# Three stages of a transformer-block kernel rewritten: the key lookup written out for all 32 batches with its head sums on TensorE, the gate sums of the recurrence on VectorE, and one power per group in the slot stage

## The reference, cut to what matters

```python
def step(h, x_t):
    score = jnp.einsum('bsh,bh->bs', enc_hiddens, h @ W)
    attn = jax.nn.softmax(score, axis=-1)
    context = jnp.einsum('bs,bsh->bh', attn, enc_hiddens)
    gx = jnp.concatenate([x_t, context], axis=-1) @ kernel + bias
    gh = h @ recurrent_kernel
    z = sigmoid(xz + hz); r = sigmoid(xr + hr)
    cand = jnp.tanh(xh + r * hh)
    h_new = z * h + (1.0 - z) * cand
```

## Time and profile before

| | |
|---|---|
| median of 3 runs | 8622.68 us |
| the profiled execution: its time / its span | 8619.14 / 8617.3 us |
| PE busy | 6440.8 us (75%) |
| DVE busy | 5008.3 us (58%) |
| ACT / POOL busy | 2976.5 us (35%) / 810.9 us (9%) |
| slot stage, four passes from 43.55 us | about 740 us |
| key-lookup passes, 817.60 to 1420.00 us | 602.4 us |
| recurrence with its block ahead, 3204 to 4586 us | about 1382 us |
| mean granted clock of TensorE (1.00 is 2.4 GHz) | 0.807 |

### The profile page before, as it was taken

How to read it: one execution, slowest core, us unless ns; L and a number is a source line. 1 busy time by engine, 2 the same in 40 slices (tenths; PEclk the granted TensorE clock), 3 DMA queues, 4 the chain that set the end, 5 groups by cost and what they waited for, 6 DMA issues and landing times. The chain is left out here.

```text
span 8617.3 us, 210690 instructions
## 1 busy us (share of the span) xinstructions
PE 6440.8 (75%) x89337; PEld 4834.8 (56%) x89337; DVE 5008.3 (58%) x17660; ACT 2976.5 (35%) x5373; POOL 810.9 (9%) x755
## 2 busy tenths in 40 slices
PE   3443223989987668998997886888888888888875
PEld 2332112767765338888886664555655556555553
DVE  4444666455455666665564336757667575775742
ACT  2222111333332222111111113545545455554541
POOL 0111222000000010000000001111011110111100
PEclk7666556999998875555557998999999999999986
DMA  1000000000000000000000000000000000000000
GB/s 29 0 0 2 0 0 25 1 1 1 1 1 4 0 3 3 4 4 4 4 4 21 0 0 17 2 9 3 2 10 2 10 2 7 5 2 10 2 4 10
DMA packets 61248, 45.12 MB, mean 5 GB/s; under 512 B 22521, under 2 KB 56125, under 8 KB 60227
## 3 DMA queue, kind: packets, MB, share of 16 engines
q1 hardware_dynamic: 60355, 32.26, 1.4%
HBM read 30.14 MB, written 2.10 MB: 4 GB/s over the span
## 5 line engine op out<-in xcount | busy, mean ns | idle before, releaser
L367 DVE TENSOR_REDUCE peak<-ps 128x8 f32<-128x1024 f32 (+1 forms) x832 | 816.9, 1024 | 270.7 <-PE ps L289 269.6
L409 ACT ACTIVATE e<-ps,H_lowT_c 77x1024 f32<-77x1024 f32 x384 | 406.0, 1106 | 253.7 <-PE ps L313 253.7
L409 ACT ACTIVATE e<-ps,H_lowT_s 128x1024 f32<-128x1024 f32 x384 | 407.3, 1112 | 248.2 <-PE ps L313 248.2
L327 PEld LDWEIGHTS ps<-e,H_vt 128*32 128x32 f32 (+1 forms) x12288 | 318.1, 111 | 254.8 <-ACT e L409 135.0
L327 PE MATMUL ps<-e,H_vt 128*32 128x128 f32 (+1 forms) x12288 | 430.3, 280 | 23.7 <-DVE xs L387 17.7
L313 PE MATMUL ps<-H_qr,H_km 32*128 32x128 f32 (+1 forms) x12288 | 420.3, 275 | 0.0
L313 PEld LDWEIGHTS ps<-H_qr,H_km 32*128 32x128 f32 (+1 forms) x12288 | 406.9, 169 | 14.8 <-issue 1.0
L1737 PE MATMUL ps<-F_hp,F_encW 128*128 128x1 bf16 (+2 forms) x12288 | 368.7, 166 | 54.2 <-issue 52.2
L1737 PEld LDWEIGHTS ps<-F_hp,F_encW 128*128 128x128 bf16 x12288 | 347.7, 104 | 55.7 <-issue 55.7
L1895 ACT ACTIVATE F_ex<-ps,F_nm 16x77 f32<-16x77 f32 x256 | 81.7, 319 | 860.6 <-DVE F_nm L1815 860.6
L1776 PE MATMUL ps<-F_eT,F_ctxp 77*128 77x1 f16 (+1 forms) x12288 | 375.6, 165 | 0.0
(11 more groups left out here) (595 smaller groups left out, 14976.6 us busy)
## 6 DMA issues: line engine op xcount, KB each, us to landing
G_w<-in_L_ffn_w SPq DMA_DIRECT2D x16, 256.0 KB
H_f<-in_L_xcond_f_w SPq DMA_DIRECT2D x12, 256.0 KB
H_nw<-in_L_xcond_n_w SPq DMA_DIRECT2D x21, 128.0 KB, 2.2
A_cond<-in_cond SPq DMA_DIRECT2D x1, 2048.0 KB
out_x<-x_all SPq DMA_DIRECT2D x1, 2048.0 KB, 8.7
ctx_rows<-in_ctx SPq DMA_DIRECT2D x1, 1232.0 KB
D_wq<-in_L_xcond_attn_wq SPq DMA_DIRECT2D x2, 512.0 KB
D_wk<-in_L_xcond_attn_wk SPq DMA_DIRECT2D x2, 512.0 KB
```

Of the source, the lines that this page charges most:

```text
L327: last = nc.tensor.matmul(ps[PAD_COLS * s:PAD_COLS * (s + 1), FLAT, r * S:(r + 1) * S], vt_of(u)[0:keys, QUAD * r + s, :], e[0:keys, half, ...
L367: last = nc.vector.tensor_reduce(peak[:, HL * half:HL * (half + 1)], view, AX.X, ALU.max, negate=True)
L409: nc.scalar.activation(e[0:keys, half, :], ps[0:keys, AGAIN[half]:AGAIN[half] + 2, :].rearrange("p b t -> p (b t)"), ACT.Exp, bias=low(u) ...
```

## The change

- Slot stage: one power of 4 columns for each group instead of one of 8 for both; VectorE normalises both groups in all norms, and ScalarE none; the softmax is subtract (VectorE, 77x512), one exponential per group (ScalarE), and sum, reciprocal, multiply, add (VectorE, each over the whole group).
- Key lookup: one Block with all 32 batches written out; `lengths(N + 1)` stands ahead of `choose(N)` on VectorE and `invert(N + 1)` ahead of `multiply(N)` on GpSimd; the sum over heads is eight accumulating identity matmuls and one for the tail (`sum_heads`); layer norm, expert activations and residual of a group are placed inside the batches of its neighbours (`nT`, `act_g` twice).
- Recurrence: RUN is 32 (four passes); `of_token` goes, VectorE adds the token's part to the gates (`gate_sums`), one tanh of 32 columns makes both gates, the bias is added once in the block ahead; three `of_state` matmuls move ahead of `turn_weights`; GpSimd copies all token inputs into place; in the block ahead the weights' parts are split early and GpSimd clears `encW` last.

```diff
-                                nc.vector.tensor_scalar(veps2[0:rows], mv2[0:rows, :, :, 1], LN_EPS, None, ALU.add).then_inc(sem["var_ready"], 1)
-                                dve.wait_ge(sem["rstd_ready"], r + 1)
-                                for j in range(1 if shared else 2):
+                                for j in range(2):
+                                    nc.vector.tensor_scalar(vepss[j][0:rows], mvs[j][0:rows, :, 1], LN_EPS, None, ALU.add).then_inc(sem["var_ready"], 1)
+                                for j in range(2):
+                                    dve.wait_ge(sem["rstd_ready"], at(r, j))
...
-                                    for u in range(U):
-                                        last = nc.scalar.activation(attns[j][:, u, :], per(bank(j, 2))[0:CL, u, :], ACT.Exp, bias=ams[j][:, u:u + 1],
-                                                                    scale=float(D) ** 0.5, accum_out=ars[j][:, u:u + 1])
+                                    nc.scalar.activation(attns[j][:], attns[j][:], ACT.Exp, scale=float(D) ** 0.5).then_inc(sem["exp_done"], 1)
...
+                        def sum_heads(N):
+                            b = N % 2
+                            pe.wait_ge(sem["outer_ready"], N + 1)
+                            pe.wait_ge(sem["tail_ready"], N + 1)
+                            if N:
+                                pe.wait_ge(sem["expert_ready"], N)
+                            for h in range(QH):
+                                nc.tensor.matmul(ps[:, 7, 0:E], ident[:], outer[:, b, h].rearrange("p i k -> p (i k)"),
+                                                 start=(h == 0), stop=False, skip_group_check=True)
+                            nc.tensor.matmul(ps[:, 7, E - 1:E], ident[:], tail[:, b:b + 1], start=False, stop=True,
+                                             skip_group_check=True).then_inc(sem["coef_done"], 1)
...
+                        for N in range(B):
+                            g, u, b = at(N)
+                            if u == 2 and g + 1 < NG:
+                                prepare(g + 1)
+                            if N + 2 < B:
+                                scores(N + 2)
+                            if u == 0 and g:
+                                mix(g - 1)
+                            sum_heads(N)
...
-            RUN = 16
+            RUN = 32
...
-                                of_token(k)
                                 of_state(k, PRODUCTS[0:3])
                                 turn_scores(k)
                                 if k > 0:
                                     late(k - 1)
+                                of_state(k, PRODUCTS[3:4])
                                 turn_weights(k)
-                                of_state(k, PRODUCTS[3:6])
+                                of_state(k, PRODUCTS[4:6])
                                 attend(k)
...
+                            def gate_sums(k):
+                                t, c = k // CH, k % CH
...
+                                dve.wait_ge(sem["gate_done"], k + 1)
+                                nc.vector.tensor_tensor(gsum[:, c], ps[:, 4 * c + 3, 0:3 * CB].rearrange("p (i b) -> p i b", i=3),
+                                                        xloc[t // PART][:, t % PART, :, mine(c)], ALU.add).then_inc(sem["gates_summed"], 1)
...
-                                act.wait_ge(sem["gate_done"], k + 1)
-                                for i, dst in ((1, rt), (0, zt)):
-                                    nc.scalar.activation(dst[:, c, :], gate(k, i), ACT.Tanh, bias=bias[:, i:i + 1],
-                                                         scale=0.5).then_inc(sem["gate_ready"], 1)
+                                act.wait_ge(sem["gates_summed"], k + 1)
+                                nc.scalar.activation(rz[:, c], gsum[:, c, 0:2], ACT.Tanh, scale=0.5).then_inc(sem["gate_ready"], 1)
```

More of the change, by code:

```diff
@@ L594, in both, with ln @@
                                 return last
-                            def ln(r, src, rows=128, signal=None, shared=False):
+                            def ln(r, src, rows=128, signal=None):
                                 for j in range(2):
                                     for u in range(U):
-                                        last = nc.vector.bn_stats(stats2[0:rows, j, u, :], src(j, u))
+                                        last = nc.vector.bn_stats(statss[j][0:rows, u, :], src(j, u))
                                 step(last)
@@ L623, in rows_of @@
                                 return xss[j][:, u, :]
-                            ln(0, lambda j, u: ctx_tm[:, g2 * (2 * U) + j * U + u, :], rows=CL, signal="z_ready", shared=True)
+                            ln(0, lambda j, u: ctx_tm[:, g2 * (2 * U) + j * U + u, :], rows=CL, signal="z_ready")
                             dve.wait_ge(sem["zT_done"], at(0, 1))
@@ L635, in _ @@
                             for it in range(3):
-                                ln(3 * it + 2, rows_of, signal="z_ready", shared=True)
+                                ln(3 * it + 2, rows_of, signal="z_ready")
                                 for j in range(2):
@@ L658, in _ @@
                                     step(add_in(j))
-                                ln(3 * it + 3, rows_of, signal="z_ready", shared=True)
+                                ln(3 * it + 3, rows_of, signal="z_ready")
                                 for j in range(2):
@@ L1046, in _, with scores @@
-                            pe.wait_ge(sem["expert_ready"], U)
+                        def scores(N):
+                            g, u, b = at(N)
+                            z_u = nT[:, g % 2, u * S:(u + 1) * S]
+                            if N >= 2:
+                                pe.wait_ge(sem["cand_ready"], N - 1)
+                                pe.wait_ge(sem["q_read"], N - 1)
+                            lay_bias(ps[:, b, :], bkey[:])
+                            nc.tensor.matmul(ps[:, b, :], z_u, wkey[:], start=False, stop=True, skip_group_check=True)
+                            lay_bias(ps[:, 2 + b, 0:NQ], bqw[:])
+                            nc.tensor.matmul(ps[:, 2 + b, 0:NQ], z_u, wq[:], start=False, stop=True,
+                                             skip_group_check=True).then_inc(sem["scores_done"], 1)
@@ L1053, in _ @@
                             last.then_inc(sem["mix_done"], 1)
-                    rest()
+                        prepare(0)
+                        scores(0)
+                        scores(1)
+                        for N in range(B):
+                            g, u, b = at(N)
+                            if u == 2 and g + 1 < NG:
+                                prepare(g + 1)
+                            if N + 2 < B:
+                                scores(N + 2)
+                            if u == 0 and g:
+                                mix(g - 1)
+                            sum_heads(N)
+                        mix(NG - 1)
+                rest()
         if "C" in SECTIONS:
@@ L1624, in _ @@
                         step(split(step, condT[:], lambda i: hp[:, :, i], xnT[:, 0:B]))
+                        dve.wait_ge(sem["loaded"], 16 * len(loads))
+                        for n in ("c", "h"):
+                            step(split(step, gate_w[n][:], lambda i: gate_p[n][:, i, :], xnT[:, 0:3 * D]))
                         dve.wait_ge(sem["rstd_ready"], 1)
@@ L1853, in blend @@
-                                step(nc.vector.scalar_tensor_tensor(out=keep[:, c, :], in0=zt[:, c, :], scalar=1.0, in1=hist[:, t, mine(c)], op0=ALU.add, op1=ALU.mult))
+                                nc.vector.tensor_scalar(zh[:, c, :], rz[:, c, 0], 1.0, 0.5, ALU.subtract, ALU.mult)
+                                step(nc.vector.scalar_tensor_tensor(out=keep[:, c, :], in0=rz[:, c, 0], scalar=1.0, in1=hist[:, t, mine(c)], op0=ALU.add, op1=ALU.mult))
                             def state(k):
```

364 lines of the change are left out of this document (202 added, 162 removed).

## The result

The changed kernel takes 8286.98 us (median of 4 runs, 8273.48 to 8289.99) against 8631.81 for the kernel before in the same session; the ratio is 0.9599, 95% interval 0.9576 to 0.9622. Run again beside other kernels later, it gave 0.9600 (0.9573 to 0.9626). Forecast were 8318 us, a ratio of 0.965. The range of 8280 to 8375 holds the median by 7 us; the narrower one of the forecast's own rival, 8290 to 8345, does not. One execution of the kernel before, beside runs 5 to 8, was a slow one (12131 us) and is left out of their ratios.

What follows compares the result with a forecast made beforehand. Each stage had its own limit: VectorE and its waits in key lookup, half-steps and seams in the recurrence, one chain through all engines in slots. Terms -241 - 38 - 15 - 4 - 7 = -305 gave 8318 us, range 8280 to 8375.

Steps and rivals of the forecast that it cites:

- the forecast's own rival: Whole kernel: the forecast of 8318 us holds, own range 8290 to 8345; chance 0.66.
- Key lookup: Key-lookup stage: VectorE is the spine, the wait for GpSimd's power goes, head sums leave VectorE; 602.4 to 361 us, -241.
- TensorE's clock: Key lookup: granted clock, 0.57 before, taken midway between low and full; group wait 1.4 us, 10 us in all.
- Seams: Recurrence: four passes instead of eight, each seam between passes costing 9.4 us; -38 us.
- Half-step: Recurrence: the token's matmul was hidden but for 0.06 us, times 256 half-steps; -15 us, to 4.82 us each.
- Block ahead: Block ahead of the recurrence: eight splits leave the end, GpSimd's clearing leaves the start; -4 us, of 0 to -8.
- Slot stage: Slot passes: norms -32 us by one power per group, softmax +25 us; net -7 us, of -30 to +15.
- The rule against it: Slot stage and key lookup: a GpSimd power shuts VectorE out for its length; +48 + 38, 8404 us, chance 0.03.
- low clock that costs in each batch: Key lookup: TensorE stays at the low clock, each batch waits some 0.25 us; +27, 8345 us, chance 0.12.
- addition on the cycle: Recurrence: VectorE's add of the token's part joins the half-step's cycle; +15 + 54, 8387 us, chance 0.10.
- growing seam: Recurrence: seams between passes grow with the loop body, so fewer passes save nothing; 8356 us, chance 0.05.
- wait for `gate_done` with the weights behind it: Recurrence: VectorE waits for `gate_done` with the weights queued behind; slower than before, 8690 us if 2 us later, chance 0.03.

Runs made afterwards that it cites:

- run 5: Changed kernel with the token's matmul back on PE and without VectorE's addition; recurrence 1283.2 us, half-step 4.86, ratio 0.9659 to the kernel before.
- run 6: Changed kernel with three state products behind the turn of the weights again; recurrence 1253.1 us, half-step 4.73, ratio 0.9616 to the kernel before.
- run 7: Changed kernel with the key lookup's sum over heads on VectorE again; key-lookup passes 401.1 us, ratio 0.9717 to the kernel before.
- run 8: Changed kernel with each batch's lengths right ahead of its own scaling, not one batch ahead; key-lookup passes 462.8 us, ratio 0.9746 to the kernel before.
- run 3: Changed kernel with recurrence passes of 16 steps instead of 32; recurrence 1295.0 us, half-step 4.73, ratio 0.9667 to the kernel before.
- run 10: Changed kernel with the token's gates on PE again and a zero bias on the candidate's tanh; recurrence 1287.9 us, half-step 4.88, ratio 0.9645 to the kernel before.
- run 4: Changed kernel with a column of zeros as bias operand of the candidate's tanh; recurrence 1276.3 us, half-step 4.82, ratio 0.9663 to the kernel before.
- run 2: Changed kernel with GpSimd's clearing first and one group split ahead of the power, not two; block ahead 58.9 us, ratio 0.9631 to the kernel before.

## Why the prediction was right, point by point

The sum was 40 us short: -305 us forecast, -346 in the two profiled executions. The key lookup came out 12 us faster than forecast, the recurrence 17 and the slots 9, the block ahead 6 slower, and 9 us are code that the change doesn't touch. So the mechanisms carry the forecast, while three of its four sizes were too small, all to the same side, and the median is only just in the range.

- **Key lookup, -241 forecast, -253 measured.** The mechanism was right in each part: the wait for the power went (104.6 to 1.4 us), the head sums hide on PE, regular batches wait for nothing. A group in the middle takes 40.8 us (lengths to lengths, four batches with the group's own work), where the working had 42.5: a bare batch is 9.0 to 9.3 us rather than 9.41, the group's own work some 3.1 rather than 3.45, and the wait for `prepare` 1.0 to 1.2 instead of 1.4 (9.2 us over the seven groups, where 10 were forecast). Seven times 1.7 us is the 12. The end was 1.5 us longer than the 9.6 assumed, because the last head sums ran at the low clock (3.79 us).
- **TensorE's clock.** The granted clock of the stage rose from 0.57 to 0.77, between the two levels as assumed. It still falls in about half of the batches: the head sums take 3.78 or 3.79 us in 17 of the 32, 2.05 in 9, and something between in 6. But for the last two nothing waited for them (1.0 and 6.1 us).
- **Seams, -38 forecast.** Four fewer seams at 9.5 us. But each one left is dearer by 1.2 to 1.5 us, some -33 in all. Its length does not depend on the body (run 3), so that rival falls. The trace shows the new part as an idle time of PE in the middle of a pass's first state products:

```profile
3312.09 1.44 PE L1836 MATMUL ps<-F_hp,F_encW 128*128 128x1 bf16 x48 [7.66 <-issue]
...
3315.00 0.26 PE L1844 MATMUL ps<-F_hp,F_ph 128*128 128x16 bf16 x4 [1.33 <-issue]
```

 The first wait is as in the earlier trace rows, the second is new and is there in passes of 16 and of 32 steps. It is there with the state products put back (run 6: 1.4 to 2.0 us) and with the token's matmul back (runs 5 and 10: 1.0 to 1.5), so neither of these edits makes it. PE waited for nothing that the profile shows; what it was is open.
- **Half-step, -15 forecast, -36 measured** (the mean inside a pass went from 4.88 to 4.74). This is the term that was mis-sized. The token's matmul was on the path by 0.06 us, exactly as read from the earlier trace rows: with it gone and a bias operand kept the step is the 4.82 of the forecast (run 4). The addition lay in the hole. The term that was missing is the bias operand of the tanh, 0.09 us x 256 = 23 us: the change moved the biases into the block ahead, and the prediction saw that edit only as work there. The Trainium skill has the price, in "ScalarE: Activation LUTs", section "What ACT_TABLE_LOAD costs": a pointer operand adds about 93 ns to an activation. The trace agrees: 0.31 against 0.22 us.
- **Block ahead, -4 forecast, +2.0 measured.** Of the wrong sign. The splits did leave the end, but with the clearing in its old place (run 2) that is worth 1.6 us, not 4. And GpSimd's clearing was taken for free at its new place; run 2 showed its price there, 3.6 us. The bound of "0" was no bound, since the working had only asked what the clearing delays on GpSimd and not on which VectorE operation it falls.
- **Slot stage, -7 forecast, -16 measured.** The norms bring 40 us, not 32 (0.83 each, not 0.67), and the softmax costs 19 to 24 where 25 were forecast. From the norm's last step ahead of the power to the first result of the MLP's product the norm of the traces took 10.35 us before and 9.51 after (274.09 to 284.44, 267.03 to 276.54), 0.84 less. The working followed only to the normalisation, 0.65 to 0.7.
- **The rule against it.** VectorE is not shut out by powers: 1.11 us beside one in the slot stage, 0.11 us for the clear inside one. By GpSimd's clearing it is, and then in its normalisations, not its statistics. The Trainium skill, "SBUF — State Buffer", section "Who interferes with whom", has this distinction: `tensor_scalar` can take the shared pair, an operation with at most one SBUF input outside those modes does not. For the clearing the traces agree with it (5.73 us, and 6.29 beside it for the statistics); for the power beside normalisations they don't. By the same section VectorE's small clear would not be held up in any case, so its 0.11 us is no test of the rule, and the prediction's 38 us for it did not follow from that page. What lies beside the 3.75 us of the earlier trace rows are GpSimd's copies and subtractions; beside its multiplications it is the clamp that takes 0.54 us instead of 0.17.
- **The rivals.** None came: no low clock that costs in each batch (its 2 us at the end did come, 1.5), no addition on the cycle, no growing seam, no wait for `gate_done` with the weights behind it.

## What to carry to other kernels

Before pricing an edit at nothing, ask of every instruction that it touches what the operand list was and what it is: a bias that moves out of an activation on the cycle was worth 0.09 us a half-step on top of the 0.06 of the matmul for which the edit seemed to be made. Where two chains close a cycle within 0.1 us, a part's price depends on the other parts: run each edit alone and both together, or the sum misleads. And a large GpSimd write has to be placed by what VectorE does beside it, not by when GpSimd is free: beside statistics 4.18 us cost nothing, beside normalisations 3.6, nearly half of it because PE was granted less clock after the longer wait.

## What the runs showed of the hardware

- A tanh of 128x16 takes 0.31 us with a bias operand and 0.22 without.
- A clearing of 4.18 us by GpSimd holds VectorE's normalisations up until it ends (5.73 us instead of 1.11) and its statistics not at all (6.29 beside it in run 2, 6.29 at 1149.87 in the changed kernel with GpSimd idle). Powers of 1.0 us don't hold up normalisations, nor powers of 2.9 us a small clear.
- After 4.09 us of waiting PE did the same turn and product at a granted clock of 0.67, after 2.11 us at 1.00 (1.09 and 3.96 us against 0.63 and 2.74).
- After a loop's turn PE can stand idle twice for "issue", 7.2 to 8.0 us ahead of its first matmul and, in the kernels with the changed body alone, 1.0 to 2.0 us a few matmuls later.
- The same untouched stage took 1268 to 1278 us at a granted clock of 0.96 in eleven kernels, 1281 and 1287 at 0.95, and 1303 at 0.94.
